# First block of a two-layer gated cross-attention kernel: the start-up work in another order

## The reference

```
x = x + tanh(g_xattn[0]) * cross_attention_0(layernorm(x), ctx, mask per batch)   # 16 heads of 16
x = x + tanh(g_ffn[0])   * switch_head_attention(layernorm(x))                    # 16 heads, 8 experts, top 2
x = x + tanh(g_xattn[1]) * cross_attention_1(layernorm(x), ctx, additive mask)
x = x + tanh(g_ffn[1])   * mixture_of_experts(layernorm(x))                       # 12 experts, top 3
```

## Time and profile before

| | |
|---|---|
| time, median of 3 runs | 1342.09 us |
| the three runs | 1334.37, 1343.16, 1342.09 us |
| profiled execution | 1335.52 us |
| its span in the trace | 1333.8 us |
| TensorE matmul busy | 1137.5 us (85%) |
| VectorE busy | 1101.4 us (83%) |
| ScalarE busy | 885.7 us (66%) |
| mean granted TensorE clock | 0.949 |
| first scores of the first block | 51.47 us |
| last update of x in the first block | 200.58 us |
| start of the second block's matmuls | 204.79 us |

### The profile page before, as it was taken

One profiled execution on the slowest core, in us unless ns is written; L12 is line 12 of the kernel. 1 busy time (PEld: TensorE's weight loads), 2 busy tenths in 40 slices (PEclk: granted clock), 3 DMA queues, 4 the chain that ended last, 5 costly groups with the idle time before them and its releaser, 6 DMA issues. The chain is left out here.

```text
span 1333.8 us, 34600 instructions
## 1 busy us (share of the span) xinstructions
PE 1137.5 (85%) x13167; PEld 929.9 (70%) x13167; DVE 1101.4 (83%) x2341; ACT 885.7 (66%) x2039; POOL 367.5 (28%) x358
## 2 busy tenths in 40 slices
PE   2788866898999989999876777767999999999996
PEld 1666753676776767768645666644889989999895
DVE  6788876899999999998745888866888888888884
ACT  1898862586776767767715988732777777777772
POOL 7122201000000000000032222002366666666763
PEclk9999988899999999999988999756999999999999
DMA  7422201334335343353222222008677788888870
GB/s 224 111 74 59 61 23 44 96 80 110 115 79 156 74 108 115 82 152 75 69 75 74 74 59 60 25 0 274 217 237 231 233 241 237 241 239 243 232 204 3
DMA packets 209042, 170.31 MB, mean 128 GB/s; under 512 B 85661, under 2 KB 190274, under 8 KB 208882
## 3 DMA queue, kind: packets, MB, share of 16 engines
q1 hardware_dynamic: 193650, 146.88, 37.0%
q0 software_dynamic: 15232, 21.26, 7.5%
HBM read 126.13 MB, written 42.86 MB: 127 GB/s over the span
## 5 line engine op out<-in xcount | busy, mean ns | idle before, releaser
L1993 POOL DMA_INDIRECT out<-m_yo,m_xg x70 | 162.2, 2317 | 133.4 <-DVE m_yo L2109 118.3
L2015 ACT ACTIVATE m_hf<-m_ps,m_bue 128x256 f32<-128x256 f32 x280 | 117.3, 471 | 106.9 <-PE m_ps L84 106.9
L1181 ACT ACTIVATE f_pr<-f_ps,f_nb 128x256 f32<-128x256 f32 x256 | 108.0, 478 | 72.2 <-DVE f_nb L1464 71.7
L82 PE MATMUL m_ps<-m_ds,m_hs 128*128 128x256 f16 x560 | 152.6, 273 | 0.3 <-DVE m_yo L2109 0.3
L84 PE MATMUL m_ps<-m_ds,m_hs 128*128 128x256 f16 x560 | 152.6, 273 | 0.0
L83 PE MATMUL m_ps<-m_ds,m_hs 128*128 128x256 f16 x560 | 152.6, 273 | 0.0
L83 PE MATMUL m_ps<-m_xt,m_us 128*128 128x256 f16 x560 | 152.6, 273 | 0.0
L82 PE MATMUL m_ps<-m_xt,m_us 128*128 128x256 f16 x560 | 152.6, 273 | 0.0
L84 PE MATMUL m_ps<-m_xt,m_us 128*128 128x256 f16 x560 | 152.6, 273 | 0.0
L723 PE MATMUL x_ps<-ident,x_pr 128*120 128x128 f32 x512 | 82.3, 285 | 40.4 <-DVE x_pt L808 29.8
L1672 DVE SCALAR_TENSOR_TENSOR m_ds<-m_draw,m_ds 128x2048 f16<-128x2048 f32 x35 | 80.2, 2292 | 41.3 <-ACT m_ds L1660 41.3
(11 more groups left out here) (386 smaller groups left out, 3872.2 us busy)
## 6 DMA issues: line engine op xcount, KB each, us to landing
m_uraw<-in_L_ffn_Wup SPq DMA_DIRECT2D x35, 1024.0 KB, 5.4
m_draw<-in_L_ffn_Wdown SPq DMA_DIRECT2D x35, 1024.0 KB, 5.8
head_values<-f_v_row SPq DMA_DIRECT2D x16, 520.0 KB, 5.1
f_vh<-head_values SPq DMA_DIRECT2D x16, 520.0 KB, 3.5
head_outputs<-f_at_row SPq DMA_DIRECT2D x16, 512.0 KB, 2.9
f_at_in_t<-head_outputs SPq DMA_DIRECT2D x16, 512.0 KB, 5.9
x_q_stack<-x_queries SPq DMA_DIRECT2D x48, 128.0 KB, 2.8
x_queries<-x_qt SPq DMA_DIRECT2D x16, 256.0 KB, 2.4
```

What stands on the lines that cost most here:

```text
L82: pe.matmul(out, lhs[0], rhs[0], start=(n == 0), stop=False)
L1181: ins = act.activation(pr[h % 2][:, ti, :], S(h)[:, ti, :], ACT.Exp, bias=nb[h % 2][:, ti:ti + 1])
L1993: pool.indirect_dma_start(rows_of, bass.IndirectOffsetOnAxis(xg[j % RING][:, ti, D:D + 1].bitcast(I32), 0), yo[j % 2][:, ti, :], None, bou ...
L2015: ins = act.activation(hf[:, q, m, :], U(q)[:, m, :], ACT.Gelu, bias=weights.bue[par][:, 2 * q + m:2 * q + m + 1], scale=UNSPLIT)
```

## The change

- VectorE's `vector` now makes the statistics and reciprocal roots of four tiles only (`FIRST_TILES = 4`, the first two batches), then the negated means of those four, then the constants (`vector_consts`). The other twelve tiles' statistics, a second round of the reciprocal roots, the second negated means, the rank constants and the gate factors stand in `vector_tiles`, behind the whole list of `XA_FIRST`.
- The low and high parts of the weights are made in two steps: key and query (`W0_FIRST`) behind the transposed context of batch 0, value and output (`W0_SECOND`) behind the transposed x of batch 0.
- SyncE's load of the second half of x goes behind the weights, the masks and the second context (`sync_late`).
- The small loads are 11: `bdown` and the causal mask go into the late loads, ahead of the second layer's weights, and the groups that wait on that semaphore wait for 7 loads instead of 5.
- The two transposes of bias rows on TensorE stand behind the first context transposes; the fill products ahead of the first two steps are left out in layer 0; the tanh of the gates goes behind `XA_FIRST`.
- Of the 17 setup groups, 11 stay ahead of the first scores; the other six (`rawo`, `raw1`) and the router's weights go into the round b == B, at u == 3.

```diff
+SMALL_LOADS = 11
+FIRST_TILES = 2 * TPB
+PROLOGUE_GROUPS = 11
...
     def vector(self, dve):
         s, ps = self.s, self.ps
         chain = Chain(dve, self.dve_step)
-        for e in range(E1):
-            dve.memset(s.rank[:, e:e + 1], float(E1 - e))
-        for tile in range(TILES):
-            if tile % (TILES // 2) == 0:
-                dve.wait_ge(self.x_loaded[tile // (TILES // 2)], 16)
+        dve.wait_ge(self.x_loaded[0], 16)
+        for tile in range(FIRST_TILES):
             tile_stats(dve, chain, s, tile)
-        rsqrt_all(dve, chain, s)
+        rsqrt_all(dve, chain, s, 0, FIRST_TILES)
+        return chain
...
+    def vector_w0(self, dve, which, made):
+        s = self.s
+        for i, n in enumerate(which):
+            dve.wait_ge(self.act_step, made + i + 1)
             dve.scalar_tensor_tensor(s.w0[n][:, 1], self.raw0[n][:], SPLIT, s.w0[n][:, 0],
                                      ALU.mult, ALU.subtract).then_inc(self.consts_made, 1)
+
+    def vector_tiles(self, dve, chain):
+        s = self.s
+        for tile in range(FIRST_TILES, TILES):
+            if tile == TILES // 2:
+                dve.wait_ge(self.x_loaded[1], 16)
+            tile_stats(dve, chain, s, tile)
+        rsqrt_all(dve, chain, s, FIRST_TILES)
+        for e in range(E1):
+            dve.memset(s.rank[:, e:e + 1], float(E1 - e))
+        dve.wait_ge(self.act_step, 5)
         dve.tensor_scalar(s.tgu[:], s.tg[:], UNSPLIT, None, ALU.mult)
...
+W0_FIRST, W0_SECOND = (1, 0), (2, 3)
+SPLIT_BEFORE = {(K_T, 0): 2, (Q_T, 0): 3, (V_, 0): 5}
...
             load(1)
+            if layer == 0:
+                setup.sync_late(sp)
...
+                if layer == 0 and n == 2:
+                    pe.wait_ge(setup.consts_made, 1)
+                if layer == 1 or n >= 2:
+                    idle_products(pe, s, ps[:, 7, :], XA_IDLE[n])
                 project(what)
+                if layer == 0 and n == 0:
+                    setup.tensor(pe)
             if layer == 0:
-                setup.tensor_late(pe)
+                setup.tensor_late(pe, 0, PROLOGUE_GROUPS)
...
                     earlier(b, u, XA_LAG, times_v)
+                    if layer == 0 and b == B and u == XA_LAG:
+                        pe.wait_ge(pt_done, XA_UNITS * B)
+                        setup.tensor_late(pe, PROLOGUE_GROUPS, len(setup.groups))
...
             for what in XA_FIRST:
                 if what[0] in (CTX_T, XN_T, V_):
                     evacuate(what)
+                if layer == 0 and what == (CTX_T, 0):
+                    setup.vector_w0(dve, W0_FIRST, 0)
+                if layer == 0 and what == (XN_T, 0):
+                    setup.vector_w0(dve, W0_SECOND, len(W0_FIRST))
                 if what[0] in (K_T, Q_T, V_) and what[1] == 0:
                     limbs(dve, chain, 0, what[0])
             if layer == 0:
-                setup.vector_late(dve)
+                setup.vector_tiles(dve, setup_chain)
+                negated(FIRST_TILES, TILES)
+                setup.vector_late(dve, 0, PROLOGUE_GROUPS)
             maxima(0, 0)
...
+                    elif u == 3 and layer == 0 and b == B:
+                        setup.vector_late(dve, PROLOGUE_GROUPS, len(setup.groups))
+                        setup.vector_gate_weights(dve)
                     elif u == 4:
```

More of the change, by code:

```diff
@@ L91, in idle_products, with rsqrt_all @@
         pe.matmul(bank, s.e16[:], s.bo16[:, 0].rearrange("p l d -> p (l d)"), start=True, stop=True)
[L94 to L98, removed]
+def rsqrt_all(dve, chain, s, first=0, end=None):
+    tiles = slice(first, TILES if end is None else end)
+    var, nt, rstd = s.var[:, tiles], s.nt[:, tiles], s.rstd[:, tiles]
+    chain(dve.tensor_scalar(var, s.mv[:, tiles, 1], EPS, None, ALU.add))
+    chain(dve.tensor_scalar(nt.bitcast(I32), var.bitcast(I32), 1, None, ALU.logical_shift_right))
+    chain(dve.tensor_scalar(rstd.bitcast(I32), nt.bitcast(I32), -1.0, RSQRT_SEED, ALU.mult, ALU.add))
     for _ in range(NEWTON_STEPS):
-        chain(dve.tensor_tensor(s.nt[:], s.rstd[:], s.rstd[:], ALU.mult))
-        chain(dve.scalar_tensor_tensor(s.nt[:], s.nt[:], -0.5, s.var[:], ALU.mult, ALU.mult))
-        chain(dve.scalar_tensor_tensor(s.rstd[:], s.nt[:], 1.5, s.rstd[:], ALU.add, ALU.mult))
+        chain(dve.tensor_tensor(nt, rstd, rstd, ALU.mult))
+        chain(dve.scalar_tensor_tensor(nt, nt, -0.5, var, ALU.mult, ALU.mult))
+        chain(dve.scalar_tensor_tensor(rstd, nt, 1.5, rstd, ALU.add, ALU.mult))
 def bf16_part(value):
@@ L247, in tensor, with tensor_late @@
                      s.ident[0:E1 * 8, 0:E1 * 8]).then_inc(self.transposed, 1)
[L248 to L252, removed]
+    def tensor_late(self, pe, first, end):
+        for g in range(first, end):
+            src, _, load = self.groups[g]
+            pe.wait_ge(self.w_loaded[load], 16 * (4, 1, 1, 1, 7)[load])
             if g >= SETUP_BANKS:
@@ L257, in tensor_late @@
             last.then_inc(self.transposed, 1)
-        pe.wait_ge(self.bank_done, len(self.groups))
+        pe.wait_ge(self.bank_done, end)
     def vector(self, dve):
@@ L652, in _ @@
                     if b + 2 < B and 1 <= u <= TPB:
+                        if layer == 0 and b == 0:
+                            act.wait_ge(nmr_ready, 2)
                         normalised_x(b + 2, u - 1)
@@ L829, in update, with negated @@
                 tile_stats(dve, chain, s, tile)
+            def negated(first, end):
+                dve.scalar_tensor_tensor(nmr[:, first:end], s.mv[:, first:end, 0], -1.0, s.rstd[:, first:end],
+                                         ALU.mult, ALU.mult).then_inc(nmr_ready, 1)
             if layer == 0:
-                setup.vector(dve)
-            dve.scalar_tensor_tensor(nmr[:], s.mv[:, :, 0], -1.0, s.rstd[:], ALU.mult, ALU.mult).then_inc(nmr_ready, 1)
+                setup_chain = setup.vector(dve)
+                negated(0, FIRST_TILES)
+                setup.vector_consts(dve, setup_chain)
+            else:
+                negated(0, TILES)
             dve.wait_ge(masks_loaded, 16)
```

65 lines of the change are left out of this document (35 added, 30 removed).

## The result

The changed kernel takes 1347.1 us (median of 20 runs), the kernel before 1342.0 (20 runs). The ratio is 1.0035, with a 95% interval from 1.002 to 1.005: some 5 us slower, clear of noise, far under 1%. One of the twenty runs took 2767.2 us, for a reason that nothing here shows; it counts in the median and not in the ratio. The profiled execution has a span of 1340.9 us, 7.1 more than before.

| us | before | after | forecast |
|---|---|---|---|
| constants begin on VectorE | 22.17 | 18.39 | 15.7 |
| keys split | 33.15 | 28.07 | 26.0 |
| values split | 40.2 | 37.6 | 33.0 |
| first setup group | 41.16 | 48.59 | 44.5 |
| first scores | 51.47 | 56.02 | 52.0 |

The account below looks back on a forecast made before the run. VectorE was taken to pace the start-up, SyncE's stacks ending 0.3 us ahead, and the block's end to be serial. +0.5 and +3.5 make +4 us: 1339.5 or 1346 by base, 1343 chosen between; range 1334 to 1350.

Parts of the forecast that it names:

- Small loads at 15.7: Start of the block: the up-bias, last small load, lands at 15.7 us and VectorE's constants begin; bounds 12.9 and 17.5.
- Constants, low parts, keys split: Start of the block: constants to 19.6 us, key low part done at 22.0, keys split from 26.0, 7 us earlier.
- 7.0 us from the keys' to the values' split: Start of the block: this stretch keeps its earlier 7.0 us with its waits, so the value split ends at 33.0.
- Twelve tiles, second links: VectorE behind the value split: 8.2 us of tiles, 2.5 of root links, 0.2 and 0.6 of small work, to 44.5.
- Eleven groups with 0.8 for the slow clock: Ahead of the first scores: 11 setup groups take 6.6 us, plus 0.8 for TensorE's slow clock, bounds 0 and 1.8.
- SyncE's chain costs nothing: Start of the block: SyncE's stores and stack loads end by 49 us, under VectorE's 52, even if the key store takes 10.
- rival 3: Start of the block: key and query stacks alone set the first scores, 7 us earlier; kernel gains 3.5 us; chance 0.05.
- End of the block, +3.5: Six groups behind the last normalisation add 3.5 us: +2.9 with TensorE's clock back, +5.0 without; floor +2.4.
- +0.5 for the start: Start of the block: first scores at 52.0 against 51.47 us, so +0.5; bounds -3.1 to +3.3.
- rival 2: Both starts at TensorE's low clock, +1.5 and +5.0, and 1.8 for late small loads: +8.3, 1344 to 1350; chance 0.2.
- Rival 1: Clock back in the tail, +2.9, and small loads early, -2.3 at the start: +0.6, 1336 to 1343; chance 0.25.

Follow-up runs that it names:

- run 1: The changed kernel with SyncE loading the second half of x ahead of the weights again; ratio 1.0027 to the kernel before.
- run 5: The changed kernel with all sixteen tiles' statistics and one round of root links in front, x loaded in the old order; ratio 1.0025 to the kernel before.
- run 6: The changed kernel with the second half of x loaded between the weights and the masks; ratio 1.0049 to the kernel before.
- run 12: The kernel before with only the six setup groups and the router's weights moved to the end of the block; ratio 1.0014 to the kernel before.
- Run 9: The changed kernel with expert bias and causal mask issued right behind the up-bias, but counted with the late loads; ratio 1.0042 to the kernel before.
- Run 4: The changed kernel with GpSimd's two casts into the query stacks ahead of its late loads; ratio 1.0058 to the kernel before.
- run 2: The changed kernel with eight instead of four tiles' statistics in front; ratio 1.0013 to the kernel before.
- run 7: The changed kernel with eight tiles in front, the other eight in batch 0's units, second root links at that batch's end; ratio 1.0025 to the kernel before.
- run 8: As run 7, but with all 17 setup groups ahead of the first scores and none at the block's end; ratio 1.0004 to the kernel before.
- experiment 10: The changed kernel itself, executed and profiled a second time; ratio 1.0063 to the kernel before, median 1350.0 us (8 runs).

## Why the prediction was right, and where its terms were off

The forecast was +4 us, 1343, with 1334 to 1350 as range; measured is +4.7 by the ratio (5 by the medians) and 1347.1. The mechanism is the one that it gave: the head start of the key chain is spent on twelve tiles in VectorE's own list, and the six groups pay at the end what they might save in front. But the sum was not right at the start of the block: first scores were forecast at 52.0, 54.8 at the latest, and came at 56.0, outside of both bounds. By its steps:

- *Small loads at 15.7.* Mis-sized: 17.6 to 19.2 in nine profiles. I took the up-bias's landing of the kernel before, 8.2 us behind its issue, for that of the changed one. About 1 us of the error is the new neighbour of the biases, the broadcast masks: the up-bias took 10.0 to 11.6 us in the nine profiles with the masks next to the weights, 9.6 to 9.9 with x ahead of them (runs 1, 5 and 6). The remaining 1.5 us is no chance of one execution: run 12, which keeps all thirteen small loads in the order of before, has 8.0 us, while runs 1 and 5, with that order and eleven loads, have 9.6. Run 9 excludes the two missing loads as the cause only in the new order (11.6 us), so it stays open. The Trainium skill's rule that was cited there (DMA: Bandwidth & Descriptors, section "Queues, rings and completion order"), that each DMA engine takes turns between the queues that have work, gave no reason to expect a loss. The trace shows one, 118 instead of 209 GB/s from 9 to 15 us; it can't tell whether the rule fails here or the turns themselves cost more beside broadcasts.
- *Constants, low parts, keys split.* 26.0 was forecast, 28.07 measured: 2.7 late from the loads, 0.6 won back. The fill products, 1.89 us for four, took 0.47 each; I had taken 0.49 from the earlier trace rows.
- *7.0 us from the keys' to the values' split.* Mis-sized by 2.6: 1.6 of it is the low part of the queries beside GpSimd's cast (2.26 for 0.69), and 0.25 the step ahead of it (0.69 for 0.43). Another 0.6 lies still ahead, on TensorE: it was still at its lower level for part of the time, and the six fill products in front of the query product took 2.09 us (1.46 before). The two rows:

```profile
27.18 2.09 PE L91 MATMUL x_ps<-bo,e 128*128 128x512 f16 x6
32.31 1.46 PE L91 MATMUL x_ps<-bo,e 128*128 128x512 f16 x6
```

The first is of the changed kernel, the second of the one before. TensorE's clock fell again behind the stretched instruction (the value products at 35.3 us took 0.42 each against 0.27 before), but that left only the last 0.2. In the kernel before the cast fell on the keys' split (1.26 us), and VectorE then still waited 1.20 us for ScalarE, so there it cost the chain little; I didn't ask what the cast would meet now. Run 4 shows the cast as the cause.

- *Twelve tiles, second links.* 11.5 forecast, 10.9 measured. This is the term that decides the sign; run 2 (-2.3 for four tiles put into idle time) and runs 7 and 8 (start 7 to 8 us earlier, with four more tiles in front and eight behind the scores) confirm it.
- *Eleven groups with 0.8 for the slow clock.* 7.5 forecast, 7.4 measured.
- *SyncE's chain costs nothing.* Right for the changed kernel, landed by 48.7, as "under 49" had it. But I missed that it is the floor for every repair (runs 5, 7, 12), and rival 3's "7 us earlier" was wrong by the same: its chain ended only 2.6 us earlier, and its store, sent 6.1 us earlier into the late weight loads, took 3.9 us longer to the next issue. What it was charged for the key store, 10 us at most, held (8.9).
- *End of the block, +3.5.* Measured +3.0 in the profile, +4.0 in the second one. Across the runs with groups at the end it was 2.95 to 4.05, in line with the two bounds that I gave, 2.9 with the clock back and 5.0 without, whose upper end was 1 us too high. Here the account was incomplete: in all ten profiles with groups at the end the clock came back during the added transposes (the last four took 0.60 to 0.63 us, 1.06 at the lower level), and the end still cost 3.3 to 4.05 in four of them (runs 2, 5, 10 and 12), because the clock had fallen again before the output product (1.48 us against 0.82). Whether it stayed up while TensorE waited for VectorE differed from profile to profile; the forecast had only asked whether it returns.

Of the sum, +0.5 for the start was the bad term: the marks give +4.5, and with the end +7.5 for the block, nearer to rival 2's +8.3 than to the +4 of the forecast. What saved the number is the range: from the profiled 1335.5 the sum gives 1339.5, while that execution was at the fast end of its kernel's runs (1334.4 to 1350.5), and the range took in both bases and rivals 1 and 2; 1347.1 lies in the 1344 to 1350 of rival 2. The ratio's +4.7 is the middle of many executions, the +7.5 that of one pair; what makes up the rest of the difference is not shown. So the number was right with a good part of luck; the sign and the size class were right by reasons. Rival 1's clock in the tail came true to the output product in six of ten profiles, without its early small loads. The Trainium skill (TensorE: Matmul & The Clock Gate, Part 1) has it that activity releases the lower level; the trace agrees with 0.50, then 1.00. Rival 2's late loads came true, and later than it had them (18.4 for 17.5), without its lasting low clock. Rival 3 is refuted.

## What to carry to other kernels

Work moved behind a critical chain is only hidden if it also stands behind the next thing that waits for its engine; read the engine's own list up to the next release, not the name of the stage. Before moving work off the front, look for the idle time it used to fill: here a wait of 4.35 us for small loads came out as soon as the statistics left it. Ask also what the moved work will run beside: a cast on another engine that cost little in one place cost 1.6 us in the next. And find the second floor first: where another chain ends only a little earlier (here SyncE's stack loads; runs 5, 7 and 12), taking work off one engine moves the end just that far.

## What the runs showed of the hardware

- Beside GpSimd's cast of 2 us from and to SBUF, a VectorE instruction of 0.29 us took 1.99, one of 0.69 took 2.26; in fourteen profiles the same key cast took 0.28 to 1.99 us. Beside GpSimd's two memsets (3.45 us together, from 8.39) a VectorE instruction on 4 elements for each partition took 1.72 us instead of 0.17 in the changed kernel (at 10.15, in time that was idle anyway), while statistics of 0.43 us beside the same memsets kept their length before (from 9.65).
- A 120 KB mask broadcast to 128 partitions beside four biases broadcast likewise went with 118 to 150 GB/s on the 16 DMA engines over six microseconds (nine profiles), against 191 to 209 with a megabyte of x between them (five profiles).
- In a half batch of 10.6 us in which TensorE was busy 8.8, its granted clock fell to a mean of 0.84, and the half batch took 1.5 us longer than at the full clock (experiment 10); the same kernel's other execution had none at that place.
- TensorE's granted clock came back within the added transposes at the end of the block (1.00 from 201 to 203 us in run 5) and was at 0.50 from 204 to 206, after a stretch in which TensorE was busy 0.33 of 2 us.
